# Second half's convolutions as 32 by 32 products, fc2's two parts on VectorE, and the order around them

## The reference

```python
def _L0_cond_ref(x, c, weight, c_weight, bias):
    out = lax.conv_general_dilated(x, weight, window_strides=(1,), padding=[(4, 4)],
        dimension_numbers=('NCH', 'OIH', 'NCH'), feature_group_count=4)
    ctx = jnp.einsum('nd,od->no', c, c_weight)
    return out + ctx[:, :, None] + bias[None, :, None]

# _L0_ffn_ref (the gate's top 2 logits are summed to one factor)
    h = jax.nn.relu(jnp.einsum('bsh,hi->bsi', hidden_states, up_w)) ** 2
    shared_out = jnp.einsum('bsi,ih->bsh', h, down_w)
    expert_out = jnp.einsum('bsl,lm->bsm', x_latent, expert_w)      # x_latent = hidden @ fc1_w
    routed_out = jnp.einsum('bsl,lh->bsh', moe_out, fc2_w)
    return _layernorm(shared_out + routed_out, ln_gamma, ln_beta)

# _L1_cond_ref
    h = gelu(gelu(embedding @ W0 + b0) @ W1 + b1)
    att = jax.nn.softmax(h @ W2 + b2, axis=-1)
    agg_w = jnp.einsum('bk,koi->boi', att, weight[..., 0])
    out = jnp.einsum('boi,bih->boh', agg_w, x) + (att @ bias_k)[:, :, None]

# reference
x = x + _L0_ffn_ref(_L0_cond_ref(...), ...)
x = x + _L1_ffn_ref(_L1_cond_ref(...), ...)
```

## Time and profile before

| | us |
|---|---|
| three runs | 222.21, 217.20, 221.17 |
| median of them | 221.17 |
| the profiled execution | 217.51 |
| its span in the profile | 215.7 |

### The profile page before, as it was taken

How to read it: one execution, slowest core, us unless ns; L and a number is a source line. 1 busy time by engine, 2 the same in 40 slices (tenths; PEclk the granted TensorE clock), 3 DMA queues, 4 the chain that set the end, 5 groups by cost and what they waited for, 6 DMA issues and landing times.

```text
span 215.7 us, 3106 instructions
## 1 busy us (share of the span) xinstructions
PE 211.2 (98%) x1155; PEld 183.4 (85%) x1155; DVE 124.8 (58%) x265; ACT 80.1 (37%) x156; POOL 61.8 (29%) x77
## 2 busy tenths in 40 slices
PE   7999899999999999999999999999999999999994
PEld 7997778888887789987888888888998998999984
DVE  4979356869525455597852034456996537435443
ACT  5998555369384612222222034431013112121110
POOL 3018421340475620021960012442264202202000
PEclk9999999999999999999999999999999999999999
DMA  6999655310000000174645000000000110110104
GB/s 177 346 406 406 219 116 109 61 27 0 0 3 0 0 0 3 25 123 68 91 41 146 0 0 0 3 0 2 0 3 0 49 49 3 50 49 0 52 0 146
DMA packets 31455, 14.94 MB, mean 69 GB/s; under 512 B 25336, under 2 KB 26168, under 8 KB 31440
## 3 DMA queue, kind: packets, MB, share of 16 engines
q1 hardware_dynamic: 30624, 14.05, 23.4%
q10 hardware_dynamic: 816, 0.69, 1.5%
HBM read 12.62 MB, written 2.11 MB: 68 GB/s over the span
## 4 chain that ended last, share of the span: by engine, by line
PE 95%; DVE 4%; issue 0%; DVEq 0%
PE PS L1214 26%; PE PS L1216 25%; PE PS L1215 25%; PE PS L1233 9%; PE PS L1341 3%; PE PS L1403 2%; DVE up_lo L864 1%; DVE H_lo L885 1%; PE PS L1258 1%; PE PS L1257 1%; PE PS L1412 1%; PE PS L1370 0%; PE PS L1267 0%; DVE ex_lo L997 0%; DVE up_hi L993 0%; PE PS L1456 0%
## 5 line engine op out<-in xcount | busy, mean ns | idle before, releaser
L910 DVE TENSOR_TENSOR PS<-PS,relu 128x512 f32<-128x512 f32 x16 | 11.2, 699 | 30.9 <-ACT relu L675 30.9
L1214 PE MATMUL PS<-H_hi,up_hi 128*128 128x512 f32 x64 | 25.6, 399 | 0.5 <-DVE H_lo L885 0.5
L1216 PE MATMUL PS<-H_hi,up_lo 128*128 128x512 f32 x64 | 25.0, 390 | 0.0
L1215 PE MATMUL PS<-H_lo,up_hi 128*128 128x512 f32 x64 | 25.0, 390 | 0.0
L1233 PE MATMUL PS<-wconv,XS 128*128 128x128 f32 x192 | 22.4, 276 | 0.0
L1233 PEld LDWEIGHTS PS<-wconv,XS 128*128 128x128 f32 x192 | 21.9, 192 | 0.3
L1216 PE MATMUL PS<-qkT_hi,H_lo 128*128 128x320 f32 x64 | 19.8, 309 | 0.0
L1215 PE MATMUL PS<-qkT_lo,H_hi 128*128 128x320 f32 x64 | 19.8, 309 | 0.0
L1214 PE MATMUL PS<-qkT_hi,H_hi 128*128 128x320 f32 x64 | 19.7, 308 | 0.0
L675 ACT ACTIVATE relu<-PS 128x512 f32<-128x512 f32 x16 | 9.5, 594 | 25.5 <-PE PS L1216 23.0
L595 POOL TENSOR_TENSOR X<-X,rowb 128x512 f32<-128x512 f32 x8 | 10.3, 1297 | 28.1 <-PE PS L1341 28.1
(11 more groups left out here) (187 smaller groups left out, 459.6 us busy)
## 6 DMA issues: line engine op xcount, KB each, us to landing
up_raw<-in_L_ffn_up_w_dram SPq DMA_DIRECT2D x2, 1024.0 KB, 8.9
dn_raw<-in_L_ffn_down_w_dram SPq DMA_DIRECT2D x2, 1024.0 KB, 13.0
out_dram<-X SPq DMA_DIRECT2D x7, 256.0 KB, 2.0
X<-in_x_dram SPq DMA_DIRECT2D x1, 1024.0 KB, 13.9
XS<-in_L_ffn_W_dram SPq DMA_DIRECT2D x16, 64.0 KB, 2.3
X<-in_x_dram SPq DMA_DIRECT2D x2, 256.0 KB, 2.9
X<-in_x_dram SPq DMA_DIRECT2D x1, 512.0 KB, 5.4
fc<-in_L_ffn_fc_w_dram SPq DMA_DIRECT2D x1, 512.0 KB, 5.7
```

Of the source, the lines that this page charges most:

```text
L910: nc.vector.tensor_tensor(U[i % 2], U[i % 2], relu[:], ALU.mult).then_inc(s_sq, 1)
L1214: nc.tensor.matmul(o, lh, rh, start=start, stop=False)
L1215: nc.tensor.matmul(o, lh, rl, start=False, stop=False)
L1216: return nc.tensor.matmul(o, ll, rh, start=False, stop=stop)
```

## The change

Four things change.

1. *The second half's convolutions.* The group matrices are gathered into `wgrp` (32 rows for each group, 32 columns) by 16 small DMAs, and reordered into `wgrp_op` by GpSimd at its third down split. X of the second half is sorted by phase in 4 copies into `wide`, written to HBM and read back into XS with the group outermost (4 and 16 DMAs). `group_convs` then does 3 windows x 4 tiles x 4 groups = 48 products of 32 x 32 weights with 512 moving columns: channels on the partitions of the result. ScalarE and VectorE add the context (`bctx`) out of the banks into `wide`, and 16 transposes (`turn_groups`) bring it into the old layout, from which H is split. `down(6)` stands between the products and the transposes. `wide` shares its memory with B1 and BD, which are filled later.
2. *The side network* runs earlier: first layer behind routed, second behind down(2), logits behind up(5), `turn_att` behind up(6), `mixing` behind down(4); exp and copies of ScalarE and VectorE move with them to chunks 4 to 6.
3. *fc2's parts* are both made by VectorE, ahead of the context rows; before, by ScalarE and GpSimd.
4. *GpSimd in the opening* waits for the first up_lo before its memsets, and copies the context rows into another order (`rows_p`); 4 DMAs write them. up_hi/up_lo of chunk 1 come after the H splits.

```diff
--- before.py
+++ after.py
...
-    ctx_rows = nc.dram_tensor("ctx_rows", [N // 2, C], F32, kind="Internal").ap()
+    ctx_rows = nc.dram_tensor("ctx_rows", [TPH * CG, SPT * G], F32, kind="Internal").ap()
+    xph_rows = nc.dram_tensor("xph_rows", [PH, C, SPT, TPH, P], F32, kind="Internal").ap()
...
+        big = sb("big", [P, 2, N * C])
+        B1 = big[:, 0]
+        BD = big[:, 1].rearrange("p (t q) -> p t q", q=P)
...
                 return [[(xs_v, v + 1)], [(xs_v, v + 2)], [(xs_v, v + 3), (xs_a, a + 1)], [(xs_a, a + 2)]][s]
-            return [(xs_v, 10), (xs_a, 7)] if T == TPH and s == 0 else []
+            return []
+        def phases(t):
+            return wide.rearrange("p j (t m) -> p j t m", t=TPH)[:, :, t], \
+                X[:, TPH + t, :].rearrange("p (m j) -> p j m", j=PH)
+        def of_sample(buf, s):
+            return buf.rearrange("m p (t s o) -> m s p t o", t=TPH, s=SPT)[:, s]
...
             sp.dma_start(rowb[:], L0_ffn_ln_beta.partition_broadcast(P)).then_inc(ld_gb, 16)
-            sp.wait_ge(s_ctx, 1)
-            sp.dma_start(ctx_rows, rows[N // 2:N]).then_inc(s_ctxw, 16)
+            sp.wait_ge(s_rowsp, 1)
+            for t in range(TPH):
+                sp.dma_start(ctx_rows[CG * t:CG * (t + 1)].rearrange("o (s g) -> s o g", g=G),
+                             rows_p[N // 2 + SPT * t:N // 2 + SPT * (t + 1)].rearrange("s (o g) -> s o g", g=G))\
+                    .then_inc(s_ctxw, 16)
             sp.wait_ge(s_fc2, 1)
...
             sp.dma_start(b2, L1_cond_b2.partition_broadcast(N)).then_inc(ld_cond, 16)
-            sp.wait_ge(s_ctxw, 16)
-            sp.dma_start(B0[:], ctx_rows.rearrange("n o -> (n o)").partition_broadcast(P)).then_inc(s_B0, 16)
+            sp.wait_ge(s_ctxw, 16 * TPH)
+            sp.dma_start(bctx.rearrange("q s g -> q (s g)"),
+                         ctx_rows.unsqueeze(1).broadcast_to([TPH * CG, PH, SPT * G])).then_inc(s_B0, 16)
+            sp.wait_ge(s_wconv, NWIN)
+            for g in range(G):
+                for j in range(PH):
+                    sp.dma_start(wgrp[C * g + CG * j:C * g + CG * (j + 1)].rearrange("k a (p o) -> k (a p) o", o=CG),
+                                 wconv[C * j + CG * g:C * j + CG * (g + 1)]
+                                 .rearrange("k a (p c) -> k (a p) c", c=C)[:, :, CG * g:CG * (g + 1)])\
+                        .then_inc(ld_wgrp, 16)
             sp.wait_ge(s_wkz, 1)
...
                 load_blocks(qk_raw[:, :, i], w, ld_qk)
+            sp.wait_ge(xs_v, 10)
+            sp.wait_ge(xs_a, 7)
+            for s in range(SPT):
+                sp.dma_start(xph_rows[:, :, s].rearrange("j c t m -> c j (t m)"), wide[C * s:C * (s + 1)])\
+                    .then_inc(s_xpw, 16)
+            sp.wait_ge(s_xpw, 16 * SPT)
+            sp.wait_ge(s_conv, TPH)
+            for g in range(G):
+                for j in range(PH):
+                    sp.dma_start(XS[C * g + CG * j:C * g + CG * (j + 1), :, 1:1 + P],
+                                 xph_rows[j, CG * g:CG * (g + 1)].rearrange("c s t m -> c (s t) m")).then_inc(ld_xs, 16)
...
             pool.wait_ge(s_foldz, 2)
-            pool.wait_ge(s_fc2h, 1)
-            nc.gpsimd.tensor_tensor(fc2_lo, fc2[:], fc2_hi.bitcast(F32), ALU.subtract).then_inc(s_fc2, 1)
+            pool.wait_ge(s_ctx, 1)
+            nc.gpsimd.tensor_copy(rows_p[:].rearrange("n (o g) -> n g o", g=G),
+                                  rows[0:N].rearrange("n (g o) -> n g o", g=G)).then_inc(s_rowsp, 1)
+            pool.wait_ge(s_up, 1)
             nc.gpsimd.memset(gate_hl[:].bitcast(mybir.dt.uint32), 0).then_inc(s_gatez, 1)
...
             nc.gpsimd.memset(cond[0:N, 384:384 + 96], 0.0).then_inc(s_att3, 1)
-            nc.gpsimd.memset(BD[:], 0.0).then_inc(s_zero, 1)
             pool.wait_ge(s_fch, 1)
...
                 split_dn(c)
+                if c == 3:
+                    pool.wait_ge(ld_wgrp, 16 * G * PH)
+                    nc.gpsimd.tensor_copy(wgrp_op.rearrange("k a (o p) -> k a p o", p=PH),
+                                          wgrp.rearrange("k a (p o) -> k a p o", p=PH)).then_inc(s_wgrp, 1)
                 if 3 <= c < 3 + TPH:
...
                 norm_scale(T)
+            pool.wait_ge(s_conv, TILES)
+            nc.gpsimd.memset(BD, 0.0).then_inc(s_zero, 1)
             pool.wait_ge(s_zero, 3)
...
                     return
-                act.wait_ge(s_tf, T - TPH + 1)
-                nc.scalar.activation(H_hi[:, :, hs], tf[:, T % 2], ACT.Copy).then_inc(s_Hh, 1)
+                act.wait_ge(s_conv, T + 1)
+                nc.scalar.activation(of_sample(H_hi[:], t), conv_bank(T).rearrange("m (t p o) -> m p t o", t=TPH, p=PH),
...
                 shift_copies(i)
-            act.wait_ge(ld_fc2, 16)
-            nc.scalar.activation(fc2_hi, fc2[:], ACT.Copy).then_inc(s_fc2h, 1)
             act.wait_ge(s_exTp, 1)
...
             split_up(0)
-            split_up(1)
             split_H(0)
...
             split_H(3)
+            split_up(1)
             act.wait_ge(ld_gate, 16)
...
                 if h:
-                    for t in range(TPH):
-                        split_H(TPH + t)
+                    act.wait_ge(s_grp, 1)
+                    act.wait_ge(s_B0, 16)
+                    for s in range(SPT):
+                        nc.scalar.activation(wide[:, 0, s * P:(s + 1) * P], conv_bank(TPH)[:, s * P:(s + 1) * P],
+                                             ACT.Identity, bias=bctx[:, s, 0:1]).then_inc(s_ga, 1)
+                    for s in range(SPT):
+                        split_H(TPH + s)
                 up_relu(i0)
...
                         split_dn(c)
-                        if c in (5, 6):
-                            hidden(c - 5)
-                        if c == 7:
-                            exp_att()
+                        if c == 4:
+                            hidden(0)
                     up_relu(i0 + c)
...
                     if h == 0 and c == 3:
-                        act.wait_ge(s_conv, TPH)
-                        shift_copies(3)
+                        act.wait_ge(ld_x[3], 16)
+                        nc.scalar.activation(*phases(2), ACT.Copy)
+                        nc.scalar.activation(*phases(3), ACT.Copy).then_inc(xs_a, 1)
+                    if h == 0 and c == 4:
+                        hidden(1)
+                        split_wk()
                     if h == 0 and c == 5:
-                        split_wk()
-                    if h == 0 and c == IC - 1:
+                        exp_att()
+                    if h == 0 and c == 6:
                         copy_attT()
...
+            dve.wait_ge(ld_fc2, 16)
+            nc.vector.tensor_copy(fc2_hi, fc2[:]).then_inc(s_fc2h, 1)
+            dve.wait_ge(s_fc2h, 1)
+            nc.vector.tensor_tensor(fc2_lo, fc2[:], fc2_hi.bitcast(F32), ALU.subtract).then_inc(s_fc2, 1)
...
                 if h:
-                    split_attT()
-                    copy_aggb()
-                    turn_agg()
+                    dve.wait_ge(s_grp, 1)
+                    dve.wait_ge(s_B0, 16)
+                    for g in range(1, G):
+                        nc.vector.tensor_tensor(wide[:, g].rearrange("q (s m) -> q s m", s=SPT),
+                                                conv_bank(TPH + g).rearrange("q (s m) -> q s m", s=SPT),
+                                                bctx[:, :, g].unsqueeze(2).broadcast_to([P, SPT, P]), ALU.add)\
+                            .then_inc(s_gv, 1)
                     for T in range(TPH, TILES):
-                        add_ctx(T)
                         split_H(T)
...
                     if h == 0 and c == 7:
-                        att_scores()
-                        att_weights()
+                        copy_aggb()
+                        turn_agg()
                     up_square(i0 + c)
...
                     if h == 0 and c == 3:
-                        shift_copies(3)
+                        dve.wait_ge(ld_x[3], 16)
+                        nc.vector.tensor_copy(*phases(0))
+                        nc.vector.tensor_copy(*phases(1)).then_inc(xs_v, 1)
+                    if h == 0 and c == 4:
+                        split_wk()
                     if h == 0 and c == 5:
-                        split_wk()
+                        att_scores()
+                        att_weights()
+                    if h == 0 and c == 6:
+                        split_attT()
                     for g in groups_after(h, c):
...
-                if T == TPH:
-                    pe.wait_ge(s_R, IC)
-                if T == TPH + 1:
-                    pe.wait_ge(s_aggb, 1)
-                if T == TPH + 2:
-                    pe.wait_ge(s_lat, LC)
...
-                if T >= TPH:
+                                                start=(a == 0 and s == 0), stop=False)
+            def group_convs():
+                pe.wait_ge(s_wgrp, 1)
+                pe.wait_ge(ld_xs, 16 * G * PH)
+                pe.wait_ge(s_R, IC)
```

(39 more changed lines are left out.)

77 lines of the change are left out of this document (31 added, 46 removed).

## The result

The changed kernel took 220.01 us (median of 10 runs, 218.16 to 221.76), the kernel before 219.47 beside it (10 runs, 217.2 to 222.21). The ratio over comparable runs is **1.0104, with a 95% interval of 1.008 to 1.0128**: 1.0% slower, less than the 2% by which verdicts go here, but outside its own uncertainty. The forecast, 214.1 in the scale of the profiled execution, was 1.6% faster; the time named was 215.5. (Five of the ten runs of the kernel before lay 3.4 to 5 us above the other five, and one of the changed kernel at 221.76; the ratio leaves these out, which is why it says more than the two medians.) The profiled execution took 220.14 with a span of 218.4, so in its scale the change is +2.7 us of span where the sum said -3.4.

What follows compares the result with a forecast made beforehand. TensorE, busy 98% of the span at full clock, was taken as the bound; opening -0.7, convolutions -5.9 and side network +3.2 gave -3.4, so 214.1 us in the profiled scale (215.5 named), range 210.0 to 224.0.

Steps and rivals of the forecast that it cites:

- All of this at no cost: DMAs for context rows, group weights and X: loads issued by 66, landed by 69, wanted at 79.7; 0 us added.
- each microsecond beyond 10 is a microsecond of TensorE: Price if the last loads of X before the tiles were late: TensorE loses 1 us per us beyond 10.
- the upper end: Top of the time range, 224.0 us: four tiles at a time in the convolutions, with the spread of the runs.
- a DMA is named before the tiles: Sign that the forecast is wrong: TensorE's wait before the tile products is named for a DMA.
- The convolutions: Second half's convolutions: 10.72 us out; tiles 2.7, two starts 0.3 and transposes 1.8 in; net -5.9 us.
- 6 rounds: Tile products: all 16 tiles run together, 3 windows x 2 instructions at 0.447 us each, 2.7 us.
- the lower end: Tile stretch of 2.7 us, out of 2.7 to 42.9, as 16 products share no array rows, columns or PSUM quadrant.
- Pairs in order: Rival: in the tiles an f32 product's second instruction waits for its first; 21.5 us, +18.8, total 232.9; chance 0.17.
- part of the overlap: Rival: only four tiles at a time (10.7 us, total 222.1) or eight (5.4 us, total 216.8); chance 0.12.
- The opening: Before the first up matmul: up(0) starts at 21.6 and not 22.33; -0.7 us, bounds 0.3 to 1.0.
- no cost, or 0.3: Wait at up(2) behind the first relu, whose context-row DMAs land perhaps 0.5 later: nothing, or 0.3 us if spare runs out.
- The side network: Earlier side network in chunks 4 to 6: waits before turn_att, before mixing and a late R(7); +3.2 us taken.

Runs made afterwards that it cites:

- wide loads: One-load version with its load cut into 16 again by sample, each 64 KB to all 128 partitions: 213.75 us, ratio 0.9833 against the kernel before.
- the cut products: One-load version with each of the 48 tile products cut into two of 256 columns, 192 instructions: 216.08 us (one run).
- the other order of the tiles: One-load version with the tile products ordered window, group, tile: 214.25 us (one run).
- the opening alone: Kernel before with only the changed opening, context rows' DMA as it was: 218.41 us (ratio 1.0035), again 218.17 us (ratio 1.0017).
- one wide load: Changed kernel with DRAM rows and group weights reordered, so X returns in one 128-partition load, not 16: 214.05 us, ratio 0.9854 against the kernel before.

## Why the prediction was wrong

**The step that failed is "All of this at no cost" in the part on the DMAs.** Its arithmetic broke at four places. *Issue:* 0.55 us apiece was taken from blocks of another shape. The 16 copies took 11.8 us and not some 9, so that the Wk blocks were through at 56.1 and not 54, and the 16 loads took 0.65 to 0.69 apiece, which is 2.2 us more up to the last. *The stores:* their landing was left out; the loads waited for it from 59.0 to 62.2. With all this the last load was issued at 72.7 and not 66. *Landing:* 3 us was allowed, and it took 9.1, since the transfers queued up behind each other at 61 to 65 GB/s. This was the one that decided: with wide loads the last was still issued at 70.4, but landed at 72.4, in time. *The date:* X was wanted at 76.9 and not 79.7, in part because the opening gained more and the waits ahead were smaller than feared; the text's own terms (78.78 less the 2.8 of down(6), -0.7, +3.2) give 78.5. The rows of before had no DMA into eight partitions, and no bound was drawn for one; "each microsecond beyond 10 is a microsecond of TensorE" named the right price, but it entered neither the sum nor a rival. That 220.0 still lies between 210.0 and 224.0 is luck: the upper end stood for tiles that overlap only in part, which didn't happen. The text itself gave "a DMA is named before the tiles" as a sign of its failure, and that sign came.

**What the wait itself would do was missing.** Even the price named was too low: a wait of 4.9 us cost 7.2, for TensorE's granted clock was 0.54 over the tiles behind it, nearly the lower level, and they took 5.66 us and not 3.33. The prediction read the granted clock as 1.00 in every stretch and let it stand for the kernel after too. Here it held until an edit opened a hole of 5 us.

**The convolutions were right in mechanism.** At full clock wait for issue, tiles and transposes take 0.2 + 3.33 + 1.8 = 5.3 us for 10.72, so -5.4 where -5.9 was forecast; the mis-sized term is the tiles, 2.7 forecast and 3.33 measured. It came from "6 rounds" of 0.447 each, as if columns bound; the cut products show that it is the number of instructions, at 34 ns each. Rounds read from the length, 7.4, mean nothing. The reason given for the lower end was wrong, too: the 16 products don't all differ in rows and columns of the array, since the four tiles of a group share its rows and the four groups of a tile its columns; the other order of the tiles shows that it costs nothing here. *Pairs in order* would have given 21.5 us and *part of the overlap* 5.4 or 10.7; the clock mimicked the second in the changed kernel (5.66), and only the runs with full clock rule it out. The page of the Trainium skill named there ("TensorE: Matmul & The Clock Gate", Part 3) says that matmuls start and end in order; the rate here doesn't contradict that, but it does contradict the reading, from which the rival was made, that an f32 pair must finish before the next tile may start. Its 10.6x would give 4.0 us, an estimate; these rows give 42.9 / 3.33 = 12.9x. The transposes (1.8) and the cover of the bias adds by down(6) came out as worked out: VectorE's three adds and ScalarE's four lie within 87.53 to 90.49, and TensorE has no wait before the transposes.

**The opening** gained 1.4 and not 0.7 in the profile. The copy of fc2 took 0.69, below the 1.1 taken and near the lower bound of 0.6, and conv_bias started at 17.18, not 17.6. That TensorE's own order would bind from there was right: the four products took until 18.20 and the twelve until 20.95. The text's own numbers, 17.6 + 0.92 + 2.8, give 21.3 and not its 21.6, so a gain of 1.0 was due by them. But of the 1.4, 0.7 was given back at up(2), which the text had at "no cost, or 0.3", and whether it arrives at all in a given execution depends on when TensorE's pace rises. So its net 0.7 agrees with the forecast by luck, and in timed runs of the opening alone the term can't be told from zero; why is partly open.

**The side network** was put at 3.2 and cost 1.5. Of its chain the head was wrong: relu(5) ran at 61.76 and not 62.8, and the table for the exp was loaded at 63.72, ahead of ScalarE's wait, so turn_att didn't wait and relu(6) ran at 67.72 and not 70.3. The text had the wait at turn_att at 0.5 with the early load and at 1.7 without, and took a sum between the two. The wait before mixing, 1.8 forecast, was 1.5, with the attT copies behind relu, square and high part as described:

```profile
63.72 1.28 ACT L794 ACT_TABLE_LOAD   x1
67.72 0.58 ACT L728 ACTIVATE relu<-PS 128x512 f32<-128x512 f32 x1
69.06 0.60 ACT L734 ACTIVATE ring<-PS 128x512 fp32r<-128x512 f32 x1 [0.76 <-DVE PS L956]
69.55 0.18 ACT L803 ACTIVATE attT<-PS 96x32 fp32r<-96x32 f32 x1
70.74 0.22 PE L1522 MATMUL PS<-bk,attT 8*32 8x32 f32 x2 [1.51 <-DVE attT L1090]
```

**Term by term:** opening -0.7 against -1.4 + 0.7; convolutions -5.9 against -5.4 at full clock; side network 3.2 against 1.5; DMAs 0 against 4.8 (the 4.97 of the empty stretch less the 0.2 already counted with the tiles), and 2.3 for the clock. Without the last two the same sum gives -4.6, and one wide load, which takes out just these, measured -3.9 of span; 0.7 of that difference isn't placed. The forecast was -3.4: the side network was 1.7 too dear, the tiles were 0.6 too cheap. So the sign of the miss lies in the term that was set to nothing, 7.1 us with its clock, and the other terms were right to within 2 us.

## What to carry to other kernels

A transfer that is "hidden anyway" needs a rate and a landing time from a row of its own shape; where the trace has none, draw a bound and let it be a rival, above all for loads into a handful of partitions, which here a reordering of the DRAM side turned into one wide load. A long wait on TensorE may cost more than itself, here 7.2 us for 4.9; look at the clock row before blaming the instructions behind it. In packed small tiles count instructions and not columns: cutting each in two nearly doubled the stretch.

## What the runs showed of the hardware

- Sixteen loads of 64 KB each ran at 63 GB/s into 8 partitions (from one block of DRAM) and at 143 GB/s into 128 (from pieces of 512 B), and cost SyncE 0.65 and 0.43 us apiece to issue.
- After 5 us without work TensorE's granted clock was 0.54 over the next 5.66 us, and full again in the stretch behind. Filler products in the wait kept it at 1.00.
- 32 by 32 tiles in plain f32, two instructions a product, run side by side: an instruction starts every 34 ns with 512 columns and with 256 alike (3.33 us for 96, 6.43 for 192), and the order of the tiles made no difference at 512.
- In some executions TensorE got through 22 instructions and not 36 from 6 to 10 us after the start, while the rows give a granted clock of 1.00. For the opening alone the two profiles are 1.6 us of span apart.
